# A four-layer mixture model on one core: products over 192 features cut as 128 and 64

## What is computed

```
# layers 0 and 1: 8 experts of 768, each token goes to its best two (layer 0 gelu with biases, layer 1 silu)
hidden = act(x @ w1[e] + b1[e]);  y = hidden @ w2[e] + b2[e];  out += share * y
# layer 2: 8 spaces of rank 16, 64 sub-experts each, the best 4 with a softmax
z = x @ P;  h = gelu(z @ W1[s, m] + b1[s, m])
comb[s] = sum_m w[s, m] * (h @ W2[s, m] + b2[s, m]);  out = gelu(comb @ G1 + g1b) @ G2 + g2b
# layer 3: 16 experts, each takes its best 204 of 1632 tokens, plus a shared expert
out[e] = (silu(xg @ Wg[e].T) * (xg @ Wu[e].T)) @ Wd[e].T * score
```

## Time and profile before

| | us |
|---|---|
| median of 3 runs (lowest, highest) | 2238.52 (2233.54, 2240.09) |
| the profiled execution | 2217.4 |
| its span | 2215.7 |
| PE busy / DVE / ACT / POOL | 1831.0 / 1252.6 / 892.4 / 356.4 |

### The profile page before, as it was taken

How to read it: one execution, slowest core, us unless ns; L and a number is a source line. 1 busy time by engine, 2 the same in 40 slices (tenths; PEclk the granted TensorE clock), 3 DMA queues, 4 the chain that set the end, 5 groups by cost and what they waited for, 6 DMA issues and landing times. The chain is left out here.

```text
span 2215.7 us, 40135 instructions
## 1 busy us (share of the span) xinstructions
PE 1831.0 (83%) x13693; PEld 1395.6 (63%) x13766; DVE 1252.6 (57%) x3619; ACT 892.4 (40%) x1938; POOL 356.4 (16%) x336
## 2 busy tenths in 40 slices
PE   5899789967775999588888559984999899749997
PEld 3678689956664999477655323332333688439997
DVE  1478822238997122478433658776788576782221
ACT  0245323314541121145332558866788355211211
POOL 0110121143211121551000000000000000223543
PEclk8999789978995899789898569986999999979998
DMA  5000356610003565110000850004000000404763
GB/s 192 1 1 0 123 138 164 164 31 16 9 25 117 146 159 132 54 37 6 0 1 0 131 102 1 1 1 78 11 1 0 22 0 0 119 24 112 180 157 60
DMA packets 68847, 139.39 MB, mean 63 GB/s; under 512 B 16803, under 2 KB 49635, under 8 KB 67683
## 3 DMA queue, kind: packets, MB, share of 16 engines
q1 hardware_dynamic: 50179, 121.03, 21.0%
q0 software_dynamic: 18528, 16.64, 3.6%
HBM read 115.37 MB, written 16.83 MB: 60 GB/s over the span
## 5 line engine op out<-in xcount | busy, mean ns | idle before, releaser
L2272 DVE TENSOR_TENSOR l2s_gated<-l2s_hidden,ps 128x408 f32<-128x408 f32 x512 | 262.7, 574 | 75.2 <-PE ps L2217 42.5
L2251 ACT ACTIVATE l2s_hidden<-ps,pack_l2f 128x408 f32<-128x408 f32 x512 | 265.9, 601 | 46.9 <-PE ps L2210 46.2
L1500 PE MATMUL ps<-l_xtT,l_up 96*128 96x128 f32 x1584 | 198.2, 284 | 3.4 <-DVE l_xtT L1761 3.4
L1500 PEld LDWEIGHTS ps<-l_xtT,l_up 96*128 96x128 f32 x1584 | 195.0, 200 | 4.7 <-DVE l_xtT L1761 4.7
L2210 PE MATMUL ps<-sub_zs,sub_up 128*128 x512 | 177.6, 348 | 20.9 <-ACTq L2246 19.0
L2217 PE MATMUL ps<-sub_gs,sub_spread 96*128 x512 | 178.1, 348 | 6.3 <-DVE l2s_gated L2272 6.0
L1511 PE MATMUL ps<-l_down,l_hidden 128*128 x792 | 140.1, 327 | 0.0
L2210 PEld LDWEIGHTS ps<-sub_zs,sub_up 128*128 128x128 bf16 x512 | 50.6, 99 | 136.4 <-ACT l2s_hidden L2251 79.3
L1511 PEld LDWEIGHTS ps<-l_down,l_hidden 128*128 128x128 f32 x792 | 128.2, 191 | 0.0
L2227 PE MATMUL ps<-l2s_gated,sub_down 128*32 128x408 f32 x1024 | 115.4, 523 | 1.2 <-DVE l2s_gated L2272 1.2
L125 PE MATMUL ps<-pack_const 128*128 128x512 bf16 x233 | 77.6, 452 | 41.2 <-PEq L159 16.2
(11 more groups left out here) (444 smaller groups left out, 3820.1 us busy)
## 6 DMA issues: line engine op xcount, KB each, us to landing
l_up<-in_l_up SPq DMA_DIRECT2D x66, 576.0 KB, 4.6
l3c_wg<-in_l_gate SPq DMA_DIRECT2D x16, 576.0 KB, 6.4
l3c_wu<-in_l_up SPq DMA_DIRECT2D x16, 576.0 KB, 8.0
l3c_wd<-in_l_down SPq DMA_DIRECT2D x16, 576.0 KB, 4.4
slots_out<-l_y SPq DMA_DIRECT2D x66, 96.0 KB
l_down<-in_l_down SPq DMA_DIRECT2D x8, 675.0 KB, 9.2
sub_gs<-l2g_g_parts SPq DMA_DIRECT2D x48, 102.0 KB, 3.1
l_down<-in_l_down SPq DMA_DIRECT2D x8, 576.0 KB, 7.0
```

Of the source, the lines that this page charges most:

```text
L1500: last = pe.matmul(hid_bank(i, half)[:, t * 128:(t + 1) * 128], up[:, i % 3, c, n * 128:(n + 1) * 128], xtT[:, i % 2, c, :], start=(c == 0 ...
L2251: act.activation(hidden[:, n % kept, :], up_bank(n), ACT.Gelu_apprx_tanh, bias=w.at("b1")[:, s * MT + t:s * MT + t + 1]).then_inc(hid_read ...
L2272: dve.tensor_tensor(gated[:, n % (2 * RG), :], hidden[:, n % kept, :], gate_bank(n), ALU.mult)\
```

## The change

Each product over 192 features is cut as 128 rows (`WIDE`) and 64 (`REST`). The parts of 64 of two neighbouring products stand side by side in the array, one on rows 0 to 63, one on rows 64 to 127 (`tile_position`). The weights are laid out on the host for that (`up`), and the turned rows of the last 64 features are written twice, by two products with the identity with 64 columns of weights each. Both halves of the hidden values of a routed tile are now signalled after its last pair. The gate products and row turns of the routed layers are cut alike, without pairs. The comparison that gives `owner` moves from behind the slots to ahead of the ranks on DVE, and POOL adds it up. There are 24, three times 2 and 24 fill products in place of 12, and one unread activation. The sub-experts lose their loop: a tile now covers both chunks, with one gelu for two banks (two pairs of up banks), and two spaces share a strip of 32 rows of the sum, 16 values each. So one chunk is in rows 0 to 63 and the other in 64 to 127 of `comb`. `sub_output` goes by four samples.

```diff
+WIDE, REST = 128, D - 128
...
+            for n, (into, other) in enumerate(((slice(0, 3), slice(3, 6)), (slice(0, 1), slice(6, 7)),
+                                               (slice(0, 1), slice(1, 2)), (slice(0, 1), slice(2, 3)))):
+                pool.wait_ge(passed_ready, n + 1)
+                pool.tensor_tensor(passed[:, into, :], passed[:, into, :], passed[:, other, :], ALU.add)\
+                    .then_inc(passed_ready, 1)
+            pool.wait_ge(passed_ready, 5)
+            pool.tensor_copy(owner[:, :], passed[:, 0, :]).then_inc(owner_ready, 1)
...
-                for c in range(C):
-                    last = pe.transpose(turned(i)[:, c * 128:(c + 1) * 128], xt[:, i % 3, c * K:(c + 1) * K], ident)
+                pe.transpose(turned(i)[:, 0:128], xt[:, i % 3, 0:WIDE], ident)
+                for twice in range(2):
+                    last = pe.matmul(turned(i)[REST * twice:REST * (twice + 1), 128:256], xt[:, i % 3, WIDE:D], ident,
+                                     start=True, stop=True, tile_position=(0, REST * twice))
...
-                for half in range(2):
-                    for t in range(3):
+                for t in range(3):
+                    for half in range(2):
                         n = 3 * half + t
-                        for c in range(C):
-                            last = pe.matmul(hid_bank(i, half)[:, t * 128:(t + 1) * 128],
-                                             up[:, i % 3, c, n * 128:(n + 1) * 128], xtT[:, i % 2, c, :],
-                                             start=(c == 0), stop=(c == C - 1))
-                    last.then_inc(hid_ps, 1)
+                        pe.matmul(hid_bank(i, half)[:, t * 128:(t + 1) * 128], up[:, i % 3, n * 128:(n + 1) * 128],
+                                  xtT[:, i % 2, 0, :], start=True, stop=False)
+                    for half in range(2):
+                        rows = slice(REST * half, REST * (half + 1))
+                        last = pe.matmul(hid_bank(i, half)[:, t * 128:(t + 1) * 128],
+                                         up[rows, i % 3, F + t * 128:F + (t + 1) * 128], xtT[rows, i % 2, 1, :],
+                                         start=False, stop=True, tile_position=(REST * half, 0))
+                        if t == 2:
+                            last.then_inc(hid_ps, 1)
 
...
+            fill(pe, g, ps[:, 0, 0, :], 24)
 
             pe.wait_ge(named_ready, 1)
             for n in range(2 * B):
                 if n % 8 == 0:
+                    if n:
+                        fill(pe, g, ps[:, 0, 0, :], 2)
...
-            fill(pe, g, ps[:, 0, 0, :], 12)
+            fill(pe, g, ps[:, 0, 0, :], 24)
...
+            act.activation(unread[:, :], gap[:, :], func)
...
+            dve.tensor_tensor(passed[:, :, :], iota[0:1, 0:TILES].unsqueeze(1).broadcast_to([1, E01 - 1, TILES]),
+                              tiles_of[1][0:1, 4:3 + E01].unsqueeze(2).broadcast_to([1, E01 - 1, TILES]), ALU.is_ge)\
+               .then_inc(passed_ready, 1)
...
-            steps.done(dve.tensor_tensor(passed[:, :, :], iota[0:1, 0:TILES].unsqueeze(2).broadcast_to([1, TILES, E01]),
-                                         tiles_of[1][0:1, 4:4 + E01].unsqueeze(1).broadcast_to([1, TILES, E01]),
-                                         ALU.is_ge))
-            steps.wait()
-            steps.done(dve.tensor_reduce(ownerf[:, :], passed[:, :, :], AX.X, ALU.add))
-            steps.wait()
-            steps.done(dve.tensor_scalar(ownerf[:, :], ownerf[:, :], float(E01 - 1), None, ALU.min))
-            steps.wait()
-            dve.tensor_copy(owner[:, :], ownerf[:, :]).then_inc(owner_ready, 1)
...
-                    mine = share[:, :].rearrange("p (b r h) -> p b r h", b=GB, h=2)[:, :, :, half:half + 1]
-                    last = dve.tensor_copy(wide[:, half, :, :, :], mine.broadcast_to([L, GB, RG, HP]))
+                    mine = share[:, :].rearrange("p (b s) -> p b s", b=GB)[:, :, half * (NS // 2):(half + 1) * (NS // 2)]
+                    last = dve.tensor_copy(wide[:, half, :, :, :],
+                                           mine.unsqueeze(3).broadcast_to([L, GB, NS // 2, NR]))
...
-    ups, gates, kept = 4, 3, 6
-    order = [(2 * r + half, t, r) for half in range(2) for t in range(MT) for r in range(RG)]
+    gates, kept, group = 3, 3, 4
+    order = [(2 * (2 * half + r) + odd, t, 2 * half + r)
+             for half in range(2) for odd in range(2) for t in range(MT) for r in range(2)]
+    pairs, per_half = len(order), len(order)
...
+            def up_products(p):
+                s, t, r = order[p]
+                if p >= 2:
+                    pe.wait_ge(hid_ready, p - 1)
+                for c in range(2):
+                    last = pe.matmul(ps[:, 0, 2 * (p % 2) + c, 0:NG], up_parts[:, s, t * 128:(t + 1) * 128],
+                                     zs[:, s, chunk(c), :], start=True, stop=True)
+                last.then_inc(up_ps, 1)
+
+            def gates_spread(n):
+                s, t, r = order[n // 2]
+                if n >= gates:
+                    pe.wait_ge(gated_ready, n - gates + 1)
+                pe.matmul(gate_bank(n), spread[:, t % 8, :], gs[:, 2 * (s % 2) + t // 8, r, chunk(n % 2), :],
                           start=True, stop=True).then_inc(gate_ps, 1)
...
+            def second(n):
+                if n == per_half:
+                    pe.wait_ge(comb_ready, 1)
+                pe.wait_ge(gated_ready, n + group)
+                for at in range(n, n + group):
+                    s, t, r = order[at // 2]
+                    row = HP * (2 * (at % 2) + r % 2)
+                    last = pe.matmul(sums[row:row + HP], down[:, s, t, :], gated[:, at % (2 * group), :],
+                                     start=(s % 2 == 0 and t == 0), stop=(s % 2 == 1 and t == MT - 1))
+                if (n + group) % per_half == 0:
...
-            with pe.Fori(0, chunks) as q:
-                up_products(0, q)
-                for n in range(tiles):
-                    if n + 1 < tiles:
-                        up_products(n + 1, q)
-                    gates_spread(n, q)
-                    if n % RG == RG - 1 and n > RG:
-                        second(n - 2 * RG + 1, q)
-                second(tiles - RG, q)
+            up_products(0)
+            for p in range(pairs):
+                if p + 1 < pairs:
+                    up_products(p + 1)
+                for n in (2 * p, 2 * p + 1):
+                    gates_spread(n)
+                if p % 2 and p >= 3:
+                    second(2 * p - 6)
...
+            for p, (s, t, r) in enumerate(order):
+                act.wait_ge(up_ps, p + 1)
+                if p >= kept:
+                    act.wait_ge(gated_ready, 2 * (p - kept + 1))
+                act.activation(hidden[:, p % kept, :, :], ps[:, 0, 2 * (p % 2):2 * (p % 2) + 2, 0:NG],
+                               ACT.Gelu_apprx_tanh, bias=w.at("b1")[:, s * MT + t:s * MT + t + 1]).then_inc(hid_ready, 1)
...
+            for n in range(2 * pairs):
+                if n == per_half + group:
+                    add_sums(0)
...
+            def hidden(q):
+                rows = slice(64 * (q % 2), 64 * (q % 2 + 1))
+                if q >= 2:
+                    pe.wait_ge(h_ready, q - 1)
+                for half in range(2):
+                    last = pe.matmul(ps[0:64, 0, q % 2, 0:NG], w.at("g1", 2)[rows, half, :],
+                                     comb[rows, q // 2, half, :, :], start=(half == 0), stop=(half == 1))
+                last.then_inc(h_ps, 1)
+
+            def results(q):
+                pe.wait_ge(h_ready, q + 1)
+                if q >= 2:
+                    pe.wait_ge(added, 2 * (q - 1))
+                for pair in range(2):
+                    for b in range(2):
+                        last = pe.matmul(rows_at(q, pair)[:, b, :], hT[:, q % 2, 2 * pair + b, :], w.at("g2"),
+                                         start=True, stop=True)
+                    last.then_inc(y_ps, 1)
+
+            fill(pe, g, ps[:, 0, 2, :], 8)
+            hidden(0)
+            hidden(1)
+            for q in range(G):
+                results(q)
+                if q + 2 < G:
+                    hidden(q + 2)
 
         @block.scalar
...
+            for q in range(G):
+                four = slice(q * GB, (q + 1) * GB)
+                dve.tensor_tensor(h[:, four, :], h[:, four, :], w.at("g2b").unsqueeze(1).broadcast_to([L, GB, D]), ALU.add)\
+                   .then_inc(based, 1)
+            for q in range(G):
+                dve.wait_ge(based, q + 1)
+                for pair in range(2):
+                    dve.wait_ge(y_ps, 2 * q + pair + 1)
+                    dve.tensor_tensor(h[:, samples(q, pair), :], h[:, samples(q, pair), :], rows_at(q, pair), ALU.add)\
+                       .then_inc(added, 1)
 
...
-                for c in range(C):
-                    for a in range(2):
```

(60 more changed lines are left out.)

204 lines of the change are left out of this document (80 added, 124 removed).

## The result

The changed kernel takes 2292.8 us (median of 4 runs, 2288.3 to 2294.7) against 2236.5 for the kernel before (4 runs): a ratio of 1.0258, 95% interval 1.0237 to 1.0279. It is slower by 56 us, where 6 us faster and a range up to 2254 were forecast. Its profiled execution has a span of 2291.4.

The account below looks back on a forecast made before the run. PE was taken to bound routed tiles and chosen experts, a round between engines the sub-experts. Terms 13.2 - 9.6 - 9.0 + 2.3 - 0.5 - 5 = -8.6 gave 2208.8 us profiled, 2230 as median; range 2193 to 2254.

Parts of the forecast that it names:

- The price of a change of the cut: On PE, each switch between 128-row and 64-row products was taken to cost 0.095 us, with 0 and 0.13 for the range.
- Rival C: A change of cut costs more, with an open weight load after a drain; at 0.13 each +18, 2256 us; slower has 0.24 in all.
- Pairs share a slot: In routed tiles and chosen experts, two 64-row products side by side take one slot, 0.112 us in a tile, 0.1725 in an expert.
- Rival E: The two products of a pair run one after the other: +98 us in all, about 2328; chance 0.04.
- rival B: The change of cut is hidden for 64-row products: sum -83, at half price -46, so 2155 to 2192 us; chance 0.15.
- Routed tiles: 66 tiles: 21 slots for 26, -0.56 us, and 8 changes, +0.76; net +0.20 a tile, +13.2 us in all.
- Chosen experts: 16 experts: -2.07 us by pairs, +0.18 for turns, +1.33 for 14 changes; net -0.56 each, -9.0 in all.
- Start of the routed tiles: Two layers: fills keep the clock up, -2.65 us; earlier weight loads, -1; cut changes, +1.5; with rounding about -9.6 in all.
- The gate products and row turns: At the start of the routed layers, 16 changes of the last four samples lie on the path: +1.5 us a layer.
- Sub-experts: 124 rounds at +0.085 us, +10.5; two loop ends gone, -6.8; two half-way adds gone, -1.4; net +2.3.
- Rival D: Waits with constants are no faster: a sub-experts round takes 2.56 us, the stage 11 more, 2241 in all; chance 0.16.
- The output stage: `sub_output`, 18.40 us for 16 samples, goes by four samples in four rounds: 13 us, -5 (bounds 0 and -9).

Follow-up runs that it names:

- the grouped kernels: Wide products ahead of their pairs: in the changed kernel's routed tiles 2245.8 us; added to the kernel without cuts with another turn 2175.7, with chosen experts too 2163.9.
- the kernel without cuts: The changed kernel with every product over 192 features back as 96 and 96, the rest of the change kept: 2214.9 us, ratio 0.9916 to the kernel before.
- the parts alone: The kernel before with only the sub-experts, gates' wide copies and output changed: 2223.4 us; with only fills, table and unread activation: 2217.6 us.
- the probes: The kernel without cuts with one more unread product ahead of each of an expert's six blocks, in three shapes: ratios 1.0009, 1.0271 and 1.0214 to the kernel before.
- the control: The kernel without cuts with an unread product of 128 rows and 128 weight columns ahead of each of an expert's six blocks: ratio 1.0009 to the kernel before.
- 64-row probe: The kernel without cuts with an unread product over 64 rows ahead of each of an expert's six blocks: ratio 1.0271 to the kernel before.
- 64 columns: The kernel without cuts with an unread product over 128 rows with 64 weight columns ahead of each of an expert's six blocks: ratio 1.0214 to the kernel before.

## Why the prediction was wrong, point by point

**The price of a change of the cut** is the step that failed: 0.095 taken, 0.13 kept as the upper bound, 0.18 to 0.19 measured. I read 0.11 where the array goes over to 32-row products and 0.13 on the way out as two readings of one quantity. The first was one part of it, the wait. Behind a change a record starts in the trace together with its weight load. From the record before to it there are 0.095 of waiting; it then loads its weights while nothing streams, so the next starts 0.10 late. In the earlier trace rows that lateness stood in the time of the 24 records, and I hid a part of it by their slots: I took 0.100 for a round, from the 96-row records of the earlier trace rows, but the rounds start 0.090 apart. 0.73 less six of 0.090 is 0.19, the whole price, and it stood in the rows before the change was made. 752 changes x 0.09 are 68 us, on a sum of -8.6: +59, against +56 measured. That it comes so close is in part luck, as the sub-experts took another 7 us off and the comparison is good to some us only. Rival C named the mechanism, an open load after the drain, but took its size from the 0.13 as well, and so ended at +18. The rule of the Trainium skill that a change of mode drains TensorE ("TensorEngine Tiling (Array Packing)", Key Properties) agrees with every change looked at here, which waits 0.09 to 0.10; this wait is about half of what is paid.

**Pairs share a slot.** Right: 12 records of pairs in six slots. Rival E falls by this, rival B by the price.

**Routed tiles.** 21 slots and 8 changes were counted rightly: -0.56 + 8 x 0.185 = +0.92, measured +0.91 (5.77 - 4.86). Chosen experts: -1.89 + 14 x 0.19 = +0.77, measured +0.77.

**Start of the routed tiles.** -9.6 predicted for two layers, in three terms. Fills and table alone gave -12.7, where 2 x -6.3 were in the sum: right, and by the way that was forecast, as 2 x 2.7 us a layer came off the first two sets of up products. In the changed kernel's own profile the fills ran in part at the low clock and gave some 2 us a layer less. The gate products and row turns cost 1.5 and 2.2 us, where +1.5 a layer was counted.

**Sub-experts.** The round came out as worked out, 2.47. The total of +2.3 was wrong in sign, about -5. From the windows: 64 rounds of 2.47 make 158 of 163 us, and the same 64 rounds of 2.39 make 153 of 167.6 and 163.4. The kernel before lost 10 to 15 us a call outside plain rounds, of which I had counted the end of the loop (3.4) and an add (0.7). By the starts of the down products in both traces, 12.5 us came off between the first and the last round of the calls beyond what their plain rounds make, where 8.2 were counted, and 2.5 ahead of the first and behind the last, where nothing was. What made the excess, no run took apart. Rival D falls. The output stage took 13.90 us for 18.40, where 13 was said.

**Chances.** The forecast was faster or the same with 0.76, and slower had 0.24; the measured 2293 lies above all that was kept in the range. Its upper end, 2254, hung on a bound, 0.13, that was no bound of the price.

## What to carry to other kernels

Count the changes of the array's cut in the order of the products, and charge each with the wait and the whole weight load behind it, 0.19 us here for 128 weight columns. A pair of 64-row products saves two slots, 0.22 us in a routed tile or 0.35 in a chosen expert, and costs two changes if it stands alone, so by these prices at least two pairs must stand together to pay. Where accumulation groups share a bank, let only the first product of the bank clear it, as the grouped kernels do, and all its wide products can stand ahead of its pairs. And when a price is read from a transition, read it from the last plain start before to the first plain start after, since behind a change a record starts with its weight load. And take the slot of a dense stretch from that stretch itself.

## What else the runs showed

**A stage that no kernel here changes has two lengths.** Layer 2's attention took 339.4 us in the profile of before and 356.0 in that of after, with the same 2055 PE records. The same stretch of 50 us, 100 us into it, before, and in the kernel without cuts:

```profile
988.90:1038.90 50.00, 44.87 (x574) 38.33 (x582) 41.20 (x119) 27.17 (x54) 8.67 (x10) 1.00 0.02 6
```

```profile
987.80:1037.80 50.00, 40.01 (x419) 34.36 (x425) 32.55 (x97) 23.15 (x46) 9.96 (x11) 0.86 0.04 11
```

The granted clock is 1.00 in one and 0.86 in the other, and less work is done. The length went with the set of runs and not with the kernel. The part of this stage that works on the tiles of its attention heads (`l2a_`) took 201 to 203 us in the profile of after, in those of the set with the parts alone and in those of the probes, and 181 to 185 in that of before and in the four of the remaining set. The 17 us are most of the 20 by which the spans of the two profiles differ more (76) than the medians (56). It also fits the medians of the kernel before, 2236, 2232 and 2236 in the sets with the long stage and 2212 in the one with the short. What decides the length stays open, so only ratios to the kernel before in the same set are compared here.

**The clock stayed down in two of the probes.** With the 64-row probe the granted clock was 0.50 in these 30 us near the start of the chosen experts, with the control it was 1.00:

```profile
2003.50:2033.00 29.50, 28.90 (x184) 28.56 (x183) 6.26 (x17) 6.11 (x17) 5.87 (x4) 1.00 0.45 109
```

```profile
2012.00:2042.00 30.00, 29.40 (x83) 24.07 (x83) 2.94 (x8) 3.24 (x9) 0.00 (x0) 0.50 0.15 39
```

In both kernels, and in every other one here, it was 0.50 in the ten microseconds before the first up product. It then rose within ten in the control, and stayed at 0.50 for over 40 with either probe that changes the cut, by 64 rows or by 64 columns. So the 64-row kernel is 57 us slower than the control where its changes alone explain 34. The changed kernel has 14 changes an expert and rose within ten as well (0.80, then 1.00), so the number of changes alone doesn't do it. What does was not separated.
